# Moving eight pieces of one-time work within the first steps and the last steps of a cross-attention and quantised-FFN kernel

## The chip, the cores and the metric

The kernel runs on one core of one Trainium2 chip. The metric is the device time of one execution in microseconds (us), and the times below are medians over several executions. The engines are named as the profile names them: PE is TensorE, DVE is VectorE, ACT is ScalarE, POOL is GpSimd, and SP is SyncE, which here only starts DMAs. Each engine runs its own list of instructions in order; engines meet only at semaphores.

## The reference

Sixteen batches of 128 tokens with 512 features go through one layer. Each batch has a context of 128 rows with 256 features, of which the first 112 are the main context and the last 16 a second segment (DCA) with weights and a softmax of its own.

```python
x = x + xattn(layernorm(x), ctx)
x = x + ffn(layernorm(x), kernel, bias)

def xattn(x, y):                      # 16 heads of 32
    y_main, y_dca = y[:, :-16], y[:, -16:]
    kv_dca = y_dca @ Wkv_dca + bkv_dca
    k_dca, v_dca = ln(kv_dca[k half] per head), kv_dca[v half]
    q = ln((x @ Wq + bq) per head)
    k, v = ln((y_main @ Wk + bk) per head), y_main @ Wv + bv
    ctx = softmax(q k^T * SCALE) v + softmax(q k_dca^T * SCALE) v_dca
    return ctx @ Wo + bo

def ffn(x, kernel, bias):             # fake_quant: scale by max |.| / 127, round, scale back
    y = fake_quant(x, -1) @ fake_quant(kernel, 0) + fake_quant(bias, -1)
    return fake_quant(relu(y), -1)
```

## The kernel before, in words

**Steps.** Every engine's list is written by hand as a function `step` that is called for t = -3 to 17. In step t six batches are in work at once, each in another stage: L = t+3 (statistics of the first layernorm), A = t+2 (transposes and the products for k, q and v), N = t+1 (norm of the heads, the stacks of q and k for the scores), Bt = t (scores, maxima, exponentials, product with v), C = t-1 (output projection, second layernorm, FFN product) and D = t-2 (end of the FFN and the store). The names in the code are these letters; `A.first()` is true in step -2 alone, `N.first()` in step -1, `Bt.first()` in step 0, `C.first()` in step 1, and `final(Bt)` in step 15. From step 2 on every step is alike.

**One-time work.** Functions named `setup_...` prepare weights and constants and are called from the first steps, between the work of the batches. The change touches these:

- `setup_selectors` (ACT) copies `sel_rows` into `sel`, 128 rows of ones and zeros for each head, by which PE adds the right row of the negated maxima to the scores. PE waits for `sel_made` as the first thing of step 0.
- squares of q: ACT squares `q_raw` of batch A into `q_sq` (L843), DVE sums them by head (L1094, `qss_ready`) and turns the sums into means (L1129); ACT then takes -1/2 powers by a logarithm and an exponential (`heads`, L705 and L707), and DVE refines them (L1038 to L1041) and scales k and q (L1142 and L1146).
- `setup_columns` (ACT, L658) takes the magnitudes of two quarters of the FFN kernel; `setup_heads` (ACT, L679 and L681) is the -1/2 power for the DCA keys, `setup_scales` and `setup_dca` on DVE (L989) go on with it.
- `setup_ffn_bias` (DVE, L1015 to L1019) quantises the FFN bias in `fb_row`. It is first needed at L1238 in step 2.
- `setup_ffn(half)` (DVE, L1026 and L1027) makes one half of the FFN kernel into integers; `low_output` (DVE, L923) makes the low part of Wo, and `low_query` (L1121) the low part of q.
- `biased_keys` (DVE, L1103) adds the bias to the product for k and writes `k_raw`, for which ACT's `squared_keys` (L734) waits. In step 0, ACT's `expo(2)` (L750) stands behind that.
- `transposed_maxima` and `first_shifted` (PE, L1519, and L1433 with L1434) turn the maxima of batch Bt over and make its shifted scores for two groups of heads; ACT copies the turned maxima into `maxT` in between.
- `turn_over(into, n)` (PE, L1341) multiplies an identity n times into a bank that nobody reads.

**Products.** An FP32 product is three products of high and low parts (`split_product`, L1330): for q over four chunks, which is twelve matmuls of 512 columns, in two halves of six; for k and v over two chunks, six matmuls.

**Order within a step, PE.** Scores of groups 2 and 3 of Bt, output projection of C (L1330, `wo_hi` and `cT_hi`), transposes of k and q of N (L1507, L1512), product for k of A, maxima, first half of the product for q, shifted scores, second half, then `weigh` (L1453) and the rest of the shifted scores by turns, the FFN's transposes and product of C (L1587, L1617), scores of groups 0 and 1 of N (L1422), the transposes of the context (L1627), and the product for v of A.

## Time and profile before

| | |
|---|---|
| median of 3 runs | 357.25 us (355.57 to 361.37) |
| profiled execution | 358.21 us, of which the span of the trace is 356.4 us |
| PE busy | 326.6 us (92% of the span) |
| DVE busy | 314.6 us (88%) |
| ACT busy | 222.0 us (62%) |
| POOL busy | 173.9 us (49%) |
| mean granted TensorE clock | 0.971 |

The span runs from the first to the last instruction in the trace. A busy share is a mean over stages that have different limits, so it doesn't say which engine sets the time in a given step. The granted clock is that of TensorE, 1.0 for 2.4 GHz and 0.5 for 1.2 GHz.

### The profile page before, as it was taken

How to read it: one execution, taken by the hardware profiler on the slowest of the kernel's cores; microseconds unless marked ns; L12 is line 12 of the kernel's file. 1: busy time of each engine (PE TensorE's matmuls, PEld its weight loads, DVE VectorE, ACT ScalarE, POOL GpSimd, SP SyncE). 2: the span in 40 equal slices, each digit the busy share in tenths (PEclk: the TensorE clock that was granted, in tenths of full speed). 3: DMA queues.
4: the chain of work that ended last, by engine and by line, in shares of the span. 5: the costliest groups of instructions: out<-in, count | busy, mean ns of one | idle time of the engine just before them, and what ended most of it. 6: DMA issues, size and time to landing. Idle time of an engine off the chain costs nothing.

```text
span 356.4 us, 7623 instructions
## 1 busy us (share of the span) xinstructions
PE 326.6 (92%) x2372; PEld 257.8 (72%) x2372; DVE 314.6 (88%) x804; ACT 222.0 (62%) x444; POOL 173.9 (49%) x261
## 2 busy tenths in 40 slices
PE   6697879899999999999999999999999999987871
PEld 2354657778888878787878787878787878775640
DVE  2997998889989999999999999999999999986665
ACT  3357986356585858585858585858585856472401
POOL 6211613317282828282828383837373747372720
PEclk9999998699999999999999999999999999999895
DMA  7970334304241514242424242333333323230002
GB/s 259 272 286 3 103 111 151 115 14 136 49 148 48 175 50 149 76 159 67 151 76 147 77 137 90 125 103 118 109 120 106 121 63 120 63 125 25 30 1 88
DMA packets 36451, 38.88 MB, mean 109 GB/s; under 512 B 8760, under 2 KB 27452, under 8 KB 36412
## 3 DMA queue, kind: packets, MB, share of 16 engines
q1 hardware_dynamic: 36044, 38.14, 33.0%
q8 instruction: 19, 0.31, 0.4%
q10 hardware_dynamic: 368, 0.27, 0.3%
q14 instruction: 20, 0.16, 0.2%
HBM read 16.89 MB, written 4.72 MB: 61 GB/s over the span
## 4 chain that ended last, share of the span: by engine, by line
PE 60%; POOL 8%; DVE 5%; issue 4%; ACT 2%; DMA 1%; POOLq 0%; ACTq 0%; DVEq 0%
PE bank L1330 33%; PE bank L1453 9%; POOL finals L536 5%; PE bank L1433 3%; PE bank L1627 3%; PE bank L1434 3%; PE bank L1422 2%; PE bank L1617 2%; PE bank L1474 2%; PE bank L1507 2%; PE bank L1512 1%; POOL x_small L593 1%; DVE seg_out L1075 1%; ACT prob_store L750 1%; DVE rden L1069 1%
## 5 line engine op out<-in xcount | busy, mean ns | idle before, releaser
L517 POOL TENSOR_TENSOR k_lo<-wkv_raw,k_hi 128x448 f16<-128x448 f32 x16 | 16.8, 1047 | 110.5 <-issue 92.9
L1453 PE MATMUL bank<-v_aug,prob_store 128*128 128x66 f32 x512 | 67.9, 276 | 2.7 <-ACT prob_store L750 2.7
L1453 PEld LDWEIGHTS bank<-v_aug,prob_store 128*128 128x128 f32 x512 | 63.7, 193 | 5.2 <-ACT prob_store L750 4.0
L761 ACT ACTIVATE wkv_raw<-bank,affine 128x448 f32<-128x448 f32 (+1 forms) x32 | 22.6, 749 | 40.6 <-PE bank L1507 40.2
L1062 DVE TENSOR_REDUCE neg_max<-bank 128x4 f32<-128x448 f32 (+1 forms) x128 | 44.9, 412 | 0.3 <-PE bank L1422 0.3
L750 ACT ACTIVATE prob_store<-bank,exp_scale 128x512 f32<-128x512 f32 x64 | 41.6, 678 | 4.9 <-PE bank L1434 4.8
L536 POOL TENSOR_TENSOR finals<-seg_out 128x128 f32<-128x128 f32 x64 | 34.5, 547 | 12.5 <-DVE seg_out L1075 11.9
L1433 PE MATMUL bank<-q_stack,k_stack 128*128 128x128 f16 x256 | 33.9, 220 | 0.6 <-ACT maxT L612 0.6
L1434 PE MATMUL bank<-maxT,sel 128*128 128x128 bf16 x256 | 33.7, 219 | 0.0
L1075 DVE TENSOR_TENSOR seg_out<-bank,rden 128x256 f32<-128x256 f32 x64 | 27.2, 424 | 4.0 <-POOL finals L536 1.7
L1433 PEld LDWEIGHTS bank<-q_stack,k_stack 128*128 128x128 f16 x256 | 26.4, 104 | 5.2 <-issue 3.9
L1330 PE MATMUL bank<-wo_hi,cT_hi 128*128 128x512 f32 x64 | 26.7, 416 | 1.8 <-DVE cT_lo L1086 1.2
L1330 PE MATMUL bank<-wq_hi,xT_hi 128*128 128x512 f32 x64 | 27.7, 432 | 0.0
L1330 PE MATMUL bank<-wq_lo,xT_hi 128*128 128x512 f32 x64 | 25.3, 396 | 0.0
L1330 PE MATMUL bank<-wo_lo,cT_hi 128*128 128x512 f32 x64 | 25.3, 395 | 0.0
L1330 PE MATMUL bank<-wo_hi,cT_lo 128*128 128x512 f32 x64 | 25.3, 395 | 0.0
L1330 PE MATMUL bank<-wq_hi,xT_lo 128*128 128x512 f32 x64 | 25.2, 394 | 0.0
L1434 PEld LDWEIGHTS bank<-maxT,sel 128*128 128x128 bf16 x256 | 25.1, 98 | 0.0
L1094 DVE TENSOR_REDUCE qk_ss<-wkv_raw 112x16 f32<-112x512 f32 (+1 forms) x32 | 21.6, 677 | 2.2 <-ACT wkv_raw L843 1.9
L546 POOL TENSOR_TENSOR wq_raw<-wq_raw,fk_scale 128x512 f32<-128x512 f32 x15 | 19.3, 1286 | 6.4 <-ACT wq_raw L866 6.4
L734 ACT ACTIVATE wkv_raw<-k_raw 112x512 f32<-112x512 f32 x16 | 10.1, 631 | 19.3 <-DVE k_raw L1103 19.3
L1422 PE MATMUL bank<-k_stack,q_stack 128*128 128x128 f16 x256 | 20.3, 224 | 0.6 <-issue 0.6
(213 smaller groups left out, 893.7 us busy)
## 6 DMA issues: line engine op xcount, KB each, us to landing
x_in<-in_x SPq DMA_DIRECT2D x16, 256.0 KB, 3.2
q_stack<-q_hi SPq DMA_DIRECT2D x32, 128.0 KB, 2.1
q_stack<-q_lo SPq DMA_DIRECT2D x32, 128.0 KB, 2.1
k_stack<-k_hi SPq DMA_DIRECT2D x32, 128.0 KB, 2.1
k_stack<-k_lo SPq DMA_DIRECT2D x32, 128.0 KB, 2.1
out<-finals SPq DMA_DIRECT2D x16, 256.0 KB, 2.0
y_dcaT<-in_x SPq DMA_DIRECT2D x8, 256.0 KB, 2.9
x_res<-in_x SPq DMA_DIRECT2D x8, 256.0 KB, 2.8
```

The costliest lines, as they stand in the source:

```text
L536: g.tensor_tensor(ctx_out[:, HG * gr:HG * (gr + 1)], seg_out[:, gr % 2, :, 0], seg_out[:, gr % 2, :, 1], ALU.add).then_inc(ctx_ready.sem, 1)
L546: g.tensor_tensor(f_z, f_z, fk_scale[:], ALU.mult).then_inc(zs_ready.sem, 1)
L750: s.activation(flat(probs[:, gr % 2]), bank[4 + gr % 2][:, :], ACT.Exp, scale=exp_scale[:, 0:1]).then_inc(probs_ready.sem, 1)
L761: s.activation(n.rearrange("p (c n) -> p c n", n=P)[:, :, 0:keys], src, ACT.Identity, bias=shift, scale=gain).then_inc(n_ready.sem, 1)
L1062: v.tensor_reduce(neg_max[:, HG * gr:HG * (gr + 1), seg], s4[:, :, lo:hi], AX.X, ALU.max, negate=True).then_inc(max_ready.sem, 1)
L1075: v.tensor_tensor(seg_out[:, gr % 2], pv[:, :, 0:2 * HD].rearrange("p h (s d) -> p h s d", d=HD), rden[:, gr % 2].unsqueeze(3).to_broadcas ...
L1094: v.tensor_reduce(qk_ss[0:rows, n], grouped(sq[0:rows]), AX.X, ALU.add).then_inc(done.sem, 1)
L1330: last = mm(dst, a[:, c, 0:m], w[:, c, :], start=first, stop=c == end and a is xT_l)
L1422: last = mm(bank[4 + gr % 2][:, P * h:P * (h + 1)], q_stack[:, b.parity, h, gr], k_stack[:, b.parity, h, gr], start=True, stop=True)
L1433: mm(at, k_stack[:, Bt.parity, h, gr], q_stack[:, Bt.parity, h, gr], start=True, stop=False)
L1434: last = mm(at, sel[:, hh], maxT[:], start=False, stop=True)
L1453: last = mm(bank[6 + gr % 2][:, VW * h:VW * (h + 1)], probs[:, gr % 2, h], v_aug[:, Bt.parity, HG * gr + h], start=True, stop=True)
```

## The change

Nothing is computed in another way, and no instruction is added but three matmuls of an identity. Moved are:

1. ACT: the selectors, from the end of step -1 to step -2, between the copy of `y_dcaT` and the copies of `wq_hi`.
2. ACT, step -2: the squares of q and `setup_heads` go ahead of the magnitudes of the FFN kernel.
3. DVE, step -2: `biased_keys` goes ahead of `setup_norms` and `setup_affine`.
4. DVE: the FFN bias, from step 0 (ahead of `yT_lo`) to the end of step 1, ahead of the maxima of groups 0 and 1.
5. DVE, step 0: `setup_ffn(0)` goes ahead of `low_query` and `low_output`.
6. PE, step 0: `transposed_maxima` goes ahead of the first half of the product for q, and `first_shifted` ahead of the second half, as in the later steps.
7. PE, step 15: `turn_over(bank[3], 3)` behind `weigh(2)`.

```diff
             def setup_weights():
                 ...
                 setup_transposed()
+                setup_selectors()
                 for half in range(2):
                     act.wait_ge(wq_centred.sem, half + 1)
...
+                def squared_queries():
+                    act.wait_ge(*qraw_ready.of(A))
+                    if A.has(1):
+                        act.wait_ge(*qss_ready.of(A.back(1)))
+                    s.activation(q_sq, q_raw[:, A.parity], ACT.Square).then_inc(qsq_ready.sem, 1)
...
                         setup_squares()
                         squared_keys()
                         token_statistics()
+                        squared_queries()
+                        setup_heads()
                         setup_columns()
-                        setup_heads()
...
-                if A is not None:
-                    act.wait_ge(*qraw_ready.of(A))
-                    if A.has(1):
-                        act.wait_ge(*qss_ready.of(A.back(1)))
-                    s.activation(q_sq, q_raw[:, A.parity], ACT.Square).then_inc(qsq_ready.sem, 1)
+                if A is not None and not A.first():
+                    squared_queries()
                 if N is not None and N.first():
                     heads(A)
                     setup_wo()
                     setup_values()
                     setup_ffn()
-                    setup_selectors()
...
-                if Bt is not None and Bt.first():
-                    setup_ffn_bias()
...
                     if A.first():
                         low_queries()
+                        biased_keys()
                         setup_norms()
                         setup_affine()
-                        biased_keys()
                         setup_squares()
                 if Bt is not None and Bt.first():
+                    setup_ffn(0)
                     low_query()
                     low_output()
-                    setup_ffn(0)
...
                         head_products(A)
+                    if C is not None and C.first():
+                        setup_ffn_bias()
                     maxima(0)
                     maxima(1)
...
-                if Bt is not None and not Bt.first():
+                if Bt is not None:
                     transposed_maxima()
...
-                if Bt is not None and Bt.first():
-                    transposed_maxima()
-                if Bt is not None and not Bt.first():
+                if Bt is not None:
                     first_shifted()
...
-                if Bt is not None and Bt.first():
-                    first_shifted()
...
                     weigh(2)
+                    if final(Bt):
+                        turn_over(bank[3], 3)
```

ACT at the end of step -2 and the start of step -1, before the change. `x_norm,x_small` is the first of the three instructions of the token statistics; a line number of the changed kernel is up to seven higher for the same statement.

```order
L718 ACTIVATE x_norm,x_small<-x_in 128x512
L721 ACTIVATE x_norm,x_square<-x_in,x_small 128x512
L724 ACTIVATE x_small<-x_square,epsilon 128x1
L658 ACTIVATE prob_store<-fk_raw 128x512 x2
L679 ACTIVATE dca_small<-dca_small 128x32
L681 ACTIVATE dca_small<-dca_small 128x32
L843 ACTIVATE wkv_raw<-q_raw 128x512
L705 ACTIVATE qk_small<-qk_small 128x32
L707 ACTIVATE qk_small<-qk_small 128x32
```

The same place after the change.

```order
L719 ACTIVATE x_norm,x_small<-x_in 128x512
L722 ACTIVATE x_norm,x_square<-x_in,x_small 128x512
L725 ACTIVATE x_small<-x_square,epsilon 128x1
L741 ACTIVATE wkv_raw<-q_raw 128x512
L680 ACTIVATE dca_small<-dca_small 128x32
L682 ACTIVATE dca_small<-dca_small 128x32
L659 ACTIVATE prob_store<-fk_raw 128x512 x2
L706 ACTIVATE qk_small<-qk_small 128x32
L708 ACTIVATE qk_small<-qk_small 128x32
```

The square of q (`wkv_raw<-q_raw`) and the two instructions on `dca_small` now stand ahead of the magnitudes of `fk_raw`, and all of them stay ahead of the two of `heads` on `qk_small`.

DVE in step 0 before the change, from the last two instructions on the FFN bias on.

```order
L1018 TENSOR_SCALAR fb_row<-fb_row,fb_stat 128x512
L1019 TENSOR_SCALAR fb_row<-fb_row,fb_stat 128x512
L1086 TENSOR_TENSOR yT_lo<-y_in,yT_hi 128x224
L1086 TENSOR_TENSOR xT_lo<-bank0,xT_hi 128x512
L1062 TENSOR_REDUCE neg_max<-bank4 128x4 x2
L1062 TENSOR_REDUCE neg_max<-bank5 128x4 x2
L1186 CAST max_parts<-neg_max 128x32
L1188 TENSOR_TENSOR max_parts<-neg_max,max_parts 128x32
L1121 TENSOR_TENSOR q_lo<-wkv_raw,q_hi 128x512
L923 TENSOR_TENSOR wo_lo<-wo_raw,wo_hi 128x2048
L1026 TENSOR_TENSOR fk_raw<-fk_raw,fk_inv 128x1024
L1027 TENSOR_SCALAR fk_int<-fk_raw 128x1024
```

The same place after the change, behind the maxima of groups 0 and 1 of step -1, up to the sum for `k_raw`.

```order
L1090 TENSOR_TENSOR yT_lo<-y_in,yT_hi 128x224
L1090 TENSOR_TENSOR xT_lo<-bank0,xT_hi 128x512
L1066 TENSOR_REDUCE neg_max<-bank4 128x4 x2
L1066 TENSOR_REDUCE neg_max<-bank5 128x4 x2
L1188 CAST max_parts<-neg_max 128x32
L1190 TENSOR_TENSOR max_parts<-neg_max,max_parts 128x32
L1030 TENSOR_TENSOR fk_raw<-fk_raw,fk_inv 128x1024
L1031 TENSOR_SCALAR fk_int<-fk_raw 128x1024
L1125 TENSOR_TENSOR q_lo<-wkv_raw,q_hi 128x512
L927 TENSOR_TENSOR wo_lo<-wo_raw,wo_hi 128x2048
L1107 TENSOR_TENSOR k_raw<-bank3,bias_full 112x512
```

The FFN bias is gone from the front, and the half of the FFN kernel stands directly behind the maxima.

DVE at the change from step 1 to step 2 before, from the sum of the squares of q to the low part of the context.

```order
L1094 TENSOR_REDUCE qk_ss<-wkv_raw 128x16
L1062 TENSOR_REDUCE neg_max<-bank4 128x4 x2
L1062 TENSOR_REDUCE neg_max<-bank5 128x4 x2
L1129 TENSOR_SCALAR qk_small<-qk_ss 128x32
L1086 TENSOR_TENSOR cT_lo<-bank6,cT_hi 128x512
```

The same place after the change.

```order
L1098 TENSOR_REDUCE qk_ss<-wkv_raw 128x16
L1019 TENSOR_REDUCE fb_stat<-fb_row 128x1
L1020 TENSOR_SCALAR fb_stat<-fb_stat 128x1
L1021 RECIPROCAL fb_stat<-fb_stat 128x1
L1022 TENSOR_SCALAR fb_row<-fb_row,fb_stat 128x512
L1023 TENSOR_SCALAR fb_row<-fb_row,fb_stat 128x512
L1066 TENSOR_REDUCE neg_max<-bank4 128x4 x2
L1066 TENSOR_REDUCE neg_max<-bank5 128x4 x2
L1133 TENSOR_SCALAR qk_small<-qk_ss 128x32
L1090 TENSOR_TENSOR cT_lo<-bank6,cT_hi 128x512
```

The five instructions on the FFN bias stand between the sum of the squares and the maxima.

## Rows read from the trace of the kernel before

**Rows 1.** The chain of waits, by engine, from the page.

```profile
PE 60%; POOL 8%; DVE 5%; issue 4%; ACT 2%; DMA 1%; POOLq 0%; ACTq 0%; DVEq 0%
```

**Rows 2.** One steady step: start:end, length, busy PE, PEld, DVE, ACT, POOL, clock, DMA.

```profile
127.84:145.90 18.06, 17.81 (x143) 14.97 (x142) 17.17 (x47) 12.73 (x28) 10.42 (x15) 1.00 0.35 111
```

**Rows 3.** Timeline, ACT, steps -2 and -1: start, us, instruction, idle before it.

```profile
20.00 2.19 ACT L612 ACTIVATE wq_hi<-wq_raw 128x1024 fp32r<-128x1024 f32 x2 [4.91 <-DVE wq_raw L905]
...
29.11 1.13 ACT L658 ACTIVATE prob_store<-fk_raw 128x512 f32<-128x512 f32 x2
...
30.53 0.61 ACT L843 ACTIVATE wkv_raw<-q_raw 128x512 f32<-128x512 f32 x1
...
49.46 2.02 ACT L612 ACTIVATE sel<-sel_rows 128x1792 bf16<-128x1792 bf16 x2
```

**Rows 4.** Timeline, DVE, steps -2 and -1.

```profile
31.17 0.69 DVE L1094 TENSOR_REDUCE qk_ss<-wkv_raw 128x16 f32<-128x512 f32 x1 [1.89 <-ACT wkv_raw L843]
...
33.70 0.19 DVE L1038 SCALAR_TENSOR_TENSOR qk_small<-qk_small 128x32 f32<-128x32 f32 x1
```

**Rows 5.** Timeline, PE: steps -2, 0, 0, 2, 15 and 16.

```profile
28.85 3.60 PE L1409 MATMUL bank<-wo_raw,bv_sum 128*128 128x512 f32 x8
...
51.53 0.66 PE L1474 MATMUL bank<-ident,x_norm 128*128 128x128 f32 x4 [1.94 <-ACT sel L612]
...
64.64 2.66 PE L1453 MATMUL bank<-v_aug,prob_store 128*128 128x66 f32 x16 [1.05 <-ACT prob_store L750]
...
91.76 0.48 PE L1330 MATMUL bank<-wo_hi,cT_hi 128*128 128x512 f32 x1
...
333.95 0.40 PE L1587 MATMUL bank<-identb,f_int 128*128 128x128 bf16 x4 [0.69 <-ACT f_int L831]
...
341.68 2.41 PE L1341 MATMUL bank<-identb 128*128 128x512 bf16 x9
```

**Rows 6.** Timeline, DVE, step 0.

```profile
50.21 0.68 DVE L1015 TENSOR_REDUCE fb_stat<-fb_row 128x1 f32<-128x512 f32 x1
...
51.84 0.49 DVE L1019 TENSOR_SCALAR fb_row<-fb_row,fb_stat 128x512 f32<-128x512 f32 x1
...
56.47 1.12 DVE L1121 TENSOR_TENSOR q_lo<-wkv_raw,q_hi 128x512 f16<-128x512 f32 x1 [1.16 <-ACT q_hi L612]
57.52 3.38 DVE L923 TENSOR_TENSOR wo_lo<-wo_raw,wo_hi 128x2048 fp32r<-128x2048 f32 x1
...
62.06 0.69 DVE L1027 TENSOR_SCALAR fk_int<-fk_raw 128x1024 bf16<-128x1024 f32 x1
62.67 0.68 DVE L1103 TENSOR_TENSOR k_raw<-bank,bias_full 112x512 f32<-112x512 f32 x1
```

**Rows 7.** Timeline, DVE, step 1 and the start of step 2.

```profile
81.42 1.07 DVE L1027 TENSOR_SCALAR fk_int<-fk_raw 128x1024 bf16<-128x1024 f32 x1
...
88.93 1.41 DVE L1062 TENSOR_REDUCE neg_max<-bank 128x4 f32<-128x448 f32 x4
...
90.75 0.69 DVE L1086 TENSOR_TENSOR cT_lo<-bank,cT_hi 128x512 fp32r<-128x512 f32 x1
```

**Rows 8.** Timeline, POOL: step 1, step 2, and the last context part in step 15.

```profile
80.65 1.30 POOL L508 TENSOR_SCALAR wo_raw<-fk_raw,f_small 128x512 f32<-128x512 f32 x1
...
89.38 1.30 POOL L546 TENSOR_TENSOR wq_raw<-wq_raw,fk_scale 128x512 f32<-128x512 f32 x1 [0.43 <-ACT wq_raw L866]
...
336.46 0.89 POOL L536 TENSOR_TENSOR finals<-seg_out 128x128 f32<-128x128 f32 x1 [0.62 <-DVE seg_out L1075]
```

**Rows 9.** Busy time of stretches in steps 0 and 1, columns as in rows 2.

```profile
52.00:54.00 2.00, 2.00 (x17) 1.99 (x16) 1.86 (x5) 1.06 (x3) 0.00 (x0) 0.53 0.42 83
...
66.00:68.00 2.00, 2.00 (x15) 1.90 (x14) 1.04 (x4) 0.00 (x0) 1.33 (x3) 0.50 0.00 0
...
72.00:74.00 2.00, 2.00 (x17) 1.78 (x16) 2.00 (x4) 1.36 (x3) 0.00 (x0) 0.85 0.00 0
```

**Rows 10.** The same view near the end, steps 15 and 16.

```profile
336.00:338.00 2.00, 2.00 (x7) 0.76 (x5) 1.04 (x2) 0.87 (x2) 0.89 (x1) 0.50 0.03 12
```

More of the change, by code:

```diff
@@ L637, in setup_transposed, with setup_selectors @@
                 copy(y_dcaT[:].rearrange("p j c n -> p (j c n)"), bank[7][:, :]).then_inc(ydcaT_copied.sem, 1)
+            def setup_selectors():
+                act.wait_ge(rows_selected.sem, 1)
+                for seg, lo, hi in ((0, 0, MAIN), (1, MAIN, P)):
+                    copy(sel[:, :, lo:hi], sel_rows[:].rearrange("p (h s) -> p h s", s=2)[:, :, seg:seg + 1]
+                         .to_broadcast([P, H, hi - lo])).then_inc(sel_made.sem, 1)
             def setup_weights():
```

5 lines of the change are left out of this document (removed).

## The prediction

> **What bounds the kernel now.** I read three views. The chain of waits puts 60% of the span on PE [rows 1], so what delays PE anywhere is mostly kept to the end. The busy times of one steady step show the same more sharply: PE is busy 17.81 of 18.06 us [rows 2], and a stall that PE takes in one step is not won back in a later one, nor is a gain lost there. The change touches no steady step but the passage from step 1 to step 2, so the whole question is by how much PE enters the steady steps earlier, and what the last steps do. For that I read the timelines of ACT, DVE and PE up to 92 us side by side, asking at each idle of PE who came last, and who at each idle of that one. Three places come out. In step -2 the sum over q on DVE waits 1.89 us for ACT's squares [rows 4]. At the start of step 0 PE stands 1.94 us until ACT has written the selectors [rows 5]. Later in step 0 PE waits 1.05 us for an exponential [rows 5], which on ACT stands behind the squares of k, and those wait for `k_raw` from DVE at 62.67 [rows 6]: DVE bounds step 0, at its end at least.
>
> **Squares of q first (step -2), -1.7 us.** ACT now does the two magnitudes of the FFN kernel, 1.13 us from 29.11 on, and `setup_heads` before the squares at 30.53 [rows 3]. With the squares first they start 1.4 us earlier, and up to 1.9 us of DVE's wait [rows 4] can go, as DVE is busy until 29.3. Behind it DVE runs without a stop from the means to the scaled k, so the refinement at 33.70 [rows 4] moves with it. Next late would be ACT's powers for q and k (L705): they come behind the magnitudes now, at about 29.3 + 0.6 + 0.4 + 1.1 = 31.4, ready near 31.9, when DVE, which has the DCA scaling ahead of them, comes to need them. Next late after that is PE, whose product for the output bias ends at 32.45 [rows 5]; the first transposes it then owes are ready by 32, so PE holds back some tenths. I take 1.7 between 1.4 and 1.9. `biased_keys` ahead of the norms makes `k_raw` 1.9 us earlier and the affine columns 0.6 us later; PE needs these only in the output bias product at 28.85 [rows 5], which has 2 us to spare. That edit is zero in itself; it only lets ACT have the squares of k done in time. If the cover went, it would cost its 0.6.
>
> **Selectors and FFN bias out of step 0, -1.9 us together.** The selectors take ACT 2.02 us at 49.46 [rows 3]. In the new place ACT is idle for 4.91 us ahead of `wq_hi` [rows 3], so they cost nothing there; if that idle time were gone, `wq_hi` and with it the product for q would be late by 2 us. PE's wait of 1.94 us [rows 5] goes entirely, since the copy of `fk_inv` it needs as well ends just as the selectors begin. DVE has to follow, or nothing is won. It spends 50.21 to 52.33 on the FFN bias [rows 6], 2.12 us, just the time in which ACT is at the selectors. Without either, DVE gets the high part of y 3.6 us earlier (1.7 and 1.9). The two edits are one gain: each alone would leave the other as the bound.
>
> **Half of the FFN kernel ahead of `q_lo` (step 0), -1.1 us.** DVE waits 1.16 us for `q_hi` ahead of `q_lo` at 56.47 [rows 6], while the 1.85 us of `setup_ffn(0)` stand behind it. Put first, they fill this wait, and `k_raw` comes another 1.1 us earlier, at 58.0 in place of 62.67: -4.7 us in all. `q_lo` itself comes 0.7 us later against its neighbours; SP still has it stacked some 3 us before PE wants the scores of batch 1. POOL's work moves beside other instructions of DVE, which may shift some tenths either way. PE's order in step 0 (maxima before the first half of the product for q) gives ACT the turned maxima and so the first two exponentials sooner. I cost it at zero: PE then only waits longer for the third exponential, as `k_raw` is later than all of that. If DVE were not the bound, it would give up to 1.4 us, the six matmuls it steps ahead of.
>
> **FFN bias at the end of step 1, +2.0 us.** There it stands ahead of the maxima at 88.93 and so of the low part of the context at 90.75 [rows 7], without which PE's output projection, which started at 91.76 [rows 5], can't. The low part ended at 91.4, so 0.3 of the 2.12 us is slack: +1.8. In step 0 POOL was idle beside it. Here POOL has its product with `fk_scale` from 89.38 to 90.68 [rows 8], just where the two 512-wide instructions fall. A row on such company: `fk_int` took 0.69 us alone [rows 6] and 1.07 us beside POOL's L508 [rows 7, 8], 0.4 more. That is +2.2 as the upper value; a gap of 0.3 between the means and the low part of the context may close, which is +1.5. I take 2.0. Behind PE at that point are the transposes of k and q and all of step 2, which is why it is kept.
>
> The Trainium skill, "SBUF — State Buffer", on the shared port pair, says that a DVE instruction in a two-port mode or with two SBUF inputs and a GpSimd one exclude each other, and whichever comes second is blocked for the whole of the other. By that rule the fourth instruction on the bias would wait for POOL's product to end, about 0.65 us, and this term would be 2.4 and the sum -2.4. The longer row of `fk_int` agrees in sign; it shows 0.4, not a block for the whole 1.30 us.
>
> **Identity products in step 15, -0.1 us.** Nine of them took 2.41 us [rows 5], so three take 0.8 us with their end, in an idle time of 0.69 us [rows 5], the last 0.1 of it being overlap: no delay. What they could give is the clock: it was 0.50 at 336 to 338 us [rows 10]. But the projection of the last batch waits there for the last part of the context, which POOL finishes at 337.35 [rows 8], whatever PE's clock. At most 0.6 us, at least -0.1 (a late transpose); I take 0.1.
>
> **Sum.** -1.7 - 1.9 - 1.1 + 2.0 - 0.1 = -2.8 us. On the profiled execution's own 358.2 us that is 355.4. That execution lies 1.0 us above the median of 357.25, so I forecast 354.5. With every term at its ends it is -4.0 to -1.7. A measurement of this kernel can tell a difference of about 2% (7 us) from none, so this is "same".
>
> **Rivals.**
>
> *The clock falls in step 2 (0.20).* PE idles about 2 us there in three pieces. After the 1.94 us at the start of step 0 the granted clock was at the lower level of 1.2 GHz (0.53 over 52 to 54 [rows 9]), at which each microsecond of work costs half a microsecond more than it should. Such a stretch costs 0.9 us at least, and the long one after the wait at 64.64, more than 6 us of which 66 to 68 and 72 to 74 are shown [rows 9], 3.3. I take 1.7: sum -1.1, 356.2. Against it: between the pieces PE has dense products. The Trainium skill, "TensorE: Matmul & The Clock Gate", says in its part on the clock gate that a recently idle array gets half its pulses; by that the fall is possible in each such place, and it names none.
>
> *The clock stays up after step 0 (0.15).* The long stretch of 66 to 73 us [rows 9] follows the wait at 64.64 [rows 5]. With the selectors' stall gone, PE is busier before it. Then step 1 gains; PE alone would gain 3.3, but DVE, hardly idle there, lets 2.1 through: sum -4.9, 352.3. Against it: the wait at 64.64 grows, since PE arrives earlier than DVE.
>
> *The first term does not arrive (0.10).* The change then doesn't do what it says for step -2: PE's output bias product until 32.45 [rows 5] and ACT's list behind it take the place of the squares as the last to come, and 0.3 of 1.7 is left: sum -1.4, 355.9.
>
> *Slower (0.05).* The stall in step 2 brings the lower clock for as long as the one at 64.64 did: +3.3 on the sum, +0.5 against before, 357.7. It decides from a low stretch of over 5.6 us on, all of it PE's.
>
> **Chances and range.** The forecast has 0.50. The range reaches from the case with the clock up and the terms near their good ends (351.5) almost to the slower case (357.5). More than 2% faster would need over 7 us, which no case gives but in chance with the spread of the runs (355.57 to 361.37): 0.04. More than 2% slower has no mechanism: 0.02. The rest is 0.94.
>
> **What would show it.** In the profile after: the second sum of squares on DVE at 29.3 to 29.8 with hardly an idle; PE into step 0 at about 48 with no wait for `sel`; `k_raw` of step 0 at about 58; PE's third `weigh` at about 60 with an idle time of over 1 us ahead of it; in step 2 PE's first `wo_hi` product at 89.1, waiting for `cT_lo`, and the bias's 512-wide instructions longer than 0.49 us. The steady step stays at 18.06. It is wrong if `k_raw` is waited for by nobody in step 0, if the clock in step 2 is below 1, or if step 2's stall is under 1 us.

## The result, and the profile after

The changed kernel takes 354.8 us in the median of 11 runs (353.72 to 357.25), the kernel before 358.02 in 11 runs beside them; the ratio is 0.9925 [0.9896, 0.9953]. A second set of 12 runs gave 355.01 against 358.53, ratio 0.9947 [0.9909, 0.9984]; two of the 29 runs of the kernel before in that set were slow ones (360.25 and 361.54), which the ratio and the comparison of single runs below leave out. That is 0.5 to 0.8% faster by the ratios (0.9 to 1.0% by the medians), "same" by the 2% bound, and the forecast of 354.5 is met. The profiled span went from 356.4 to 353.0 us. The number came out right with two of its terms wrong and with TensorE's clock as a third cause, to which the forecast gave nothing; the rest of this text is about that.

The chain of waits by engine, kernel after (answers to [rows 1]):

```profile
PE 59%; POOL 8%; DVE 7%; issue 5%; ACT 2%; DMA 1%; POOLq 0%; DVEq 0%; ACTq 0%
```

PE still carries it, so the starts of PE's landmarks tell where time was won. The timeline of PE, kernel after (start, us, instruction, idle time before it and who ended it; answers to [rows 5]):

```profile
48.07 0.63 PE L1478 MATMUL bank<-ident,x_norm 128*128 128x128 f32 x4 [0.26 <-ACT fk_inv L612]
...
52.80 0.22 PE L1523 MATMUL bank<-identb,max_parts 128*128 128x128 bf16 x1 [1.45 <-DVE max_parts L1190]
...
60.36 2.00 PE L1457 MATMUL bank<-v_aug,prob_store 128*128 128x66 f32 x16 [0.83 <-ACT prob_store L757]
...
85.43 0.40 PE L1426 MATMUL bank<-k_stack,q_stack 128*128 128x128 f16 x4 [0.74 <-DVE neg_max L1066]
86.09 0.40 PE L1426 MATMUL bank<-k_stack,q_stack 128*128 128x128 f16 x4 [0.27 <-DVE neg_max L1066]
86.99 0.64 PE L1334 MATMUL bank<-wo_hi,cT_hi 128*128 128x512 f32 x1 [0.50 <-DVE cT_lo L1090]
...
335.60 0.47 PE L1334 MATMUL bank<-wo_hi,cT_hi 128*128 128x512 f32 x1 [0.88 <-DVE cT_lo L1162]
```

The reader sees the selectors' wait of 1.94 gone (0.26 is left), PE in step 0 at 48.07 in place of 51.53, the third `weigh` at 60.36 in place of 64.64, and three new idle times in step 2, 1.51 us together. DVE in steps -2 and 0, kernel after (answers to [rows 4, 6]):

```profile
28.42 1.47 DVE L1098 TENSOR_REDUCE qk_ss<-wkv_raw 112x16 f32<-112x512 f32 x2
...
31.74 0.19 DVE L1042 SCALAR_TENSOR_TENSOR qk_small<-qk_small 128x32 f32<-128x32 f32 x1
...
51.63 1.02 DVE L1190 TENSOR_TENSOR max_parts<-neg_max,max_parts 128x32 bf16<-128x32 f32 x1
52.57 2.36 DVE L1030 TENSOR_TENSOR fk_raw<-fk_raw,fk_inv 128x1024 f32<-128x1024 f32 x1
...
58.38 0.68 DVE L1107 TENSOR_TENSOR k_raw<-bank,bias_full 112x512 f32<-112x512 f32 x1
```

Both sums of squares of step -2 run without idle and the refinement comes 1.96 us earlier. `k_raw` of step 0 comes 4.29 us earlier. Two instructions there are long (`max_parts` 1.02, `fk_raw` 2.36), and POOL was busy beside them. POOL in steps 0 and 2, kernel after; the second row is its sum of x and the output bias, which stands in the buffer named `y_dca`:

```profile
51.57 1.03 POOL L517 TENSOR_TENSOR k_lo<-wkv_raw,k_hi 128x448 f16<-128x448 f32 x1 [7.29 <-issue]
52.56 1.29 POOL L583 TENSOR_TENSOR y_dca<-y_dcaT,out_bias 128x512 f32<-128x512 f32 x1
...
82.59 1.29 POOL L546 TENSOR_TENSOR wq_raw<-wq_raw,fk_scale 128x512 f32<-128x512 f32 x1 [0.42 <-ACT wq_raw L870]
```

DVE ahead of PE's idle times in step 2, kernel after (answers to [rows 7]):

```profile
82.14 0.68 DVE L1019 TENSOR_REDUCE fb_stat<-fb_row 128x1 f32<-128x512 f32 x1
...
83.24 0.92 DVE L1022 TENSOR_SCALAR fb_row<-fb_row,fb_stat 128x512 f32<-128x512 f32 x1
84.20 0.51 DVE L1023 TENSOR_SCALAR fb_row<-fb_row,fb_stat 128x512 f32<-128x512 f32 x1
84.63 1.40 DVE L1066 TENSOR_REDUCE neg_max<-bank 128x4 f32<-128x448 f32 x4
```

Last the clock. PE's busy time in stretches, kernel after (start:end, length, busy PE, granted clock, DMA share, GB/s; answers to [rows 9, 10]):

```profile
65.00:67.00 2.00, 2.00 (x19) 1.00 0.32 116
...
86.00:88.00 2.00, 1.40 (x7) 0.78 0.00 0
88.00:90.00 2.00, 2.00 (x7) 0.50 0.00 0
...
336.00:338.00 2.00, 2.00 (x10) 1.00 0.00 0
```

The lower level (1.2 GHz) after the third `weigh` of step 0 is gone; it appears in step 2, behind the new idle times, and not at 336.

**The ledger.** The starts on PE of five landmarks cut the way into stages: k product of step -1 (B), transposes of x in step 0 (C), third `weigh` of step 0 (D), first output projection product of step 1 (E), of step 2 (F), of step 16 (G). "Wait" is the idle time ahead of D. All from PE's timeline of each profiled execution, us, with the kernels of the experiments below in the same table:

| kernel | B | B to C | C to D | wait | D to E | E to F | F to G |
|---|---|---|---|---|---|---|---|
| before | 38.22 | 13.31 | 13.11 | 1.05 | 8.55 | 18.57 | 246.97 |
| after | 36.30 | 11.77 | 12.29 | 0.83 | 6.05 | 20.58 | 248.61 |
| changed_again | 38.37 | 11.86 | 12.11 | 0.65 | 6.07 | 20.59 | 247.01 |
| squares_alone | 37.03 | 13.55 | 12.39 | 0.37 | 6.06 | 18.55 | 247.30 |
| selectors_alone | 38.21 | 12.56 | 12.62 | 0.56 | 6.06 | 18.54 | 247.55 |
| bias_alone | 38.32 | 14.27 | 12.30 | 1.67 | 8.57 | 20.61 | 247.32 |
| all_but_bias | 36.56 | 11.67 | 12.75 | 0 | 6.07 | 18.56 | 247.27 |
| fk_behind | 37.10 | 11.88 | 12.24 | 0.77 | 6.05 | 20.59 | 247.07 |
| clock_held | 36.27 | 11.65 | 12.28 | 0.81 | 6.06 | 20.58 | 246.72 |
| sum_later | 36.77 | 11.85 | 11.31 | 0 | 6.08 | 20.59 | 247.14 |
| bias_back_sum_later | 37.33 | 11.83 | 11.92 | 0 | 6.06 | 18.54 | 247.06 |
| pe_order_back | 36.69 | 11.87 | 12.13 | 1.52 | 8.55 | 20.59 | 247.14 |
| no_identities | 36.28 | 11.63 | 12.11 | 0.65 | 6.07 | 20.59 | 247.11 |
| bias_on_gpsimd | 36.59 | 11.67 | 11.67 | 0.60 | 6.07 | 18.55 | 247.11 |

From before to after: -1.92 (B), -1.54 and -0.82 (step 0), -2.50 (D to E), +2.01 (E to F), +1.64 (F to G, of which 1.52 lies between F and the next k product), and -0.27 behind G, together -3.40, the difference of the spans. Two of these are clock: D to E holds the same work in 6.05 us at 1.00 and in 8.55 with the clock mostly at 0.50, and 1.52 of the +1.64 is the fall in step 2. Most of the -0.82 is clock too, as squares_alone will show.

### The profile page after: what moved, and what is told of

It is laid out like the page before. It is cut to its first block, busy times and chain, and to the rows that moved or that the text cites. A ratio compares the mean times of both kernels' runs of the same rounds, so it can differ in the third digit from the quotient of the medians.

```text
span 353.0 us, 7629 instructions
## 1 busy us (share of the span) xinstructions
PE 321.9 (91%) x2375; PEld 254.4 (72%) x2375; DVE 315.7 (89%) x804; ACT 221.9 (63%) x444; POOL 173.8 (49%) x261
## 4 chain that ended last, share of the span: by engine, by line
PE 59%; POOL 8%; DVE 7%; issue 5%; ACT 2%; DMA 1%; POOLq 0%; DVEq 0%; ACTq 0%
PE bank L1334 33%; PE bank L1457 9%; POOL finals L536 5%; PE bank L1437 3%; PE bank L1438 3%; PE bank L1629 2%; PE bank L1426 2%; PE bank L1511 2%; PE bank L1516 1%; PE bank L1478 1%; POOL x_small L593 1%; DVE seg_out L1079 1%; PE bank L1619 1%; DVE rden L1073 1%; ACT prob_store L757 1%
## 5 line engine op out<-in xcount | busy, mean ns | idle before, releaser
L1457 PE MATMUL bank<-v_aug,prob_store 128*128 128x66 f32 x512 | 67.1, 274 | 2.1 <-ACT prob_store L757 2.1
```

The source lines that it names most:

```text
L1457: last = mm(bank[6 + gr % 2][:, VW * h:VW * (h + 1)], probs[:, gr % 2, h], v_aug[:, Bt.parity, HG * gr + h], start=True, stop=True)
```

## The experiments

The first four were timed against 29 runs of the kernel before (357.5 us), the next four against 23 (356.16), the last four against 29 (358.53). Where I compare medians they are of kernels timed together, or I give both ratios.

**squares_alone**: the kernel before with the squares of q first in step -2 and the keys ahead of the norms.

```diff
                         token_statistics()
+                        squared_queries()
+                        setup_heads()
                         setup_columns()
-                        setup_heads()
```

> The kernel before with two edits alone: ACT squares q of step -2 ahead of the magnitudes of the FFN kernel, and DVE adds the bias to k ahead of the norms. Theory (the wait for the squares set step -1): the sum over q on DVE has hardly an idle, PE's product for k of step -1 starts 1.9 us earlier (36.3 in place of 38.2), PE still stands some 1.9 us at the start of step 0 for the selectors, and the whole is 1.7 to 1.9 us faster. Rival (something else comes last in step -1, PE's output bias product or ACT's list behind it): under 0.5 us.

355.27 us, ratio 0.9932 [0.9893, 0.9971]. PE's timeline in step 0:

```profile
50.58 0.66 PE L1478 MATMUL bank<-ident,x_norm 128*128 128x128 f32 x4 [1.93 <-ACT sel L612]
...
62.97 2.00 PE L1457 MATMUL bank<-v_aug,prob_store 128*128 128x66 f32 x16 [0.37 <-ACT prob_store L756]
```

B is at 37.03 and the selectors' wait stands unchanged at 1.93: the term is independent of the others. The median is 2.2 us below that of before, where 1.7 to 1.9 was expected, but D to E is 6.06 in this execution, so some of that may be clock.

This run also shows what made step 0 of the kernel before longer in its profiled execution. Step 0 holds the same lists and the same selectors' wait in both, and yet DVE's wait for `q_hi` is 0.45 here and was 1.16 there. PE and then ACT, kernel before:

```profile
52.77 0.95 PE L1507 MATMUL bank<-ident,wq_raw 112*128 112x112 f32 x4
```

```profile
53.76 1.63 ACT L761 ACTIVATE wkv_raw<-bank,affine 128x448 f32<-128x448 f32 x2 [0.94 <-PE bank L1507]
```

The same for squares_alone, and its DVE:

```profile
51.52 0.56 PE L1511 MATMUL bank<-ident,wq_raw 112*128 112x112 f32 x4
```

```profile
52.11 1.62 ACT L767 ACTIVATE wkv_raw<-bank,affine 128x448 f32<-128x448 f32 x2 [0.24 <-PE bank L1511]
```

```profile
54.80 1.12 DVE L1125 TENSOR_TENSOR q_lo<-wkv_raw,q_hi 128x512 f16<-128x512 f32 x1 [0.45 <-ACT q_hi L612]
```

In the kernel before the clock had fallen (0.53 over 52 to 54 us) by the time of the transposes of k. They took 0.95 us in place of 0.56, ACT waited 0.94 in place of 0.24, and `q_hi`, `q_lo`, `k_raw` and the third `weigh` each came 0.7 us later behind the start of step 0 (C to D 13.11 against 12.39). In squares_alone the clock fell as well (0.50 over 52 to 54 us), but behind those transposes. So 0.7 of the 1.16 us, and 0.7 of the 1.05 us ahead of D, were the clock. Over all kernels with this edit B lies at 36.27 to 38.37, the middle one at 36.69, and at 38.21 to 38.32 in the three without.

**selectors_alone**: the kernel before with `setup_selectors()` behind `setup_transposed()` alone.

```diff
                 setup_transposed()
+                setup_selectors()
...
                     setup_ffn()
-                    setup_selectors()
```

> The kernel before with one edit alone: the selectors are written in step -2. Theory (DVE is the bound of step 0 once PE's wait is gone, since the FFN bias still keeps it until 52.3): PE starts step 0 about 1.6 to 1.9 us earlier, but the k_raw of step 0 on DVE stays within 0.5 us of 62.7, and the time within 0.5 us of before as long as the granted clock does the same; PE just waits longer for the third exponential. Rival (PE's wait was the bound): k_raw at about 60.8 and the whole 1.9 us faster. If the clock does not fall at the start of step 1 any more, up to 2.5 us come off in either case, and then only the place of k_raw decides between the two.

354.45 us, ratio 0.9915 [0.9883, 0.9948]: 3.0 us below the median of before, of which D to E (6.06) is 2.5 in the profiled executions. DVE has no wait for `q_hi`, and `k_raw` is at 61.41 in place of 62.67, beyond the 0.5 us that were expected. B to D is 25.18 against 26.42, and against 25.94 in squares_alone, where the clock did not make the transposes late: 0.8 us less with the FFN bias still in step 0, and that with a mean clock of 0.91 over 30 to 48 us. So this edit alone earns something, and the forecast's "each alone would leave the other as the bound" falls.

**bias_alone**: the kernel before with only the FFN bias moved to the end of step 1.

```diff
-                if Bt is not None and Bt.first():
-                    setup_ffn_bias()
...
+                    if C is not None and C.first():
+                        setup_ffn_bias()
                     maxima(0)
```

> The kernel before with one edit alone: the FFN bias goes from step 0 to the end of step 1. Theory (in step 0 DVE then waits for ACT, which is at the selectors, so nothing is won there; at the end of step 1 it delays the low part of the context): k_raw of step 0 stays within 0.5 us of 62.7, PE's output projection of step 2 waits about 2 us, and the whole is 2.0 us slower, up to 3.6 if the clock falls in that wait. Rival (each edit earns its own time): k_raw 2 us earlier, and the whole within 0.5 us of before.

359.68 us, ratio 1.0049 [1.0007, 1.009]: slower beyond the interval, "same" by the 2% bound. B to D is 26.57, with a clock of 0.50 to 0.94 over 36 to 42 us in it, and E to F is 20.61 in place of 18.57. DVE ahead of the low part of y, and PE at the third `weigh`:

```profile
53.40 0.39 DVE L1086 TENSOR_TENSOR yT_lo<-y_in,yT_hi 128x224 fp32r<-128x224 f32 x1 [1.98 <-issue]
```

```profile
64.89 3.53 PE L1453 MATMUL bank<-v_aug,prob_store 128*128 128x66 f32 x16 [1.67 <-ACT prob_store L750]
```

With the selectors still there, the 2.12 us that DVE saves come back as 1.98 of waiting. This half of the forecast's sentence is true: the bias alone earns nothing in step 0 and costs 2.0 in step 2.

**all_but_bias**: the changed kernel with the bias back in step 0.

```diff
+                if Bt is not None and Bt.first():
+                    setup_ffn_bias()
...
-                    if C is not None and C.first():
-                        setup_ffn_bias()
                     maxima(0)
```

> The changed kernel with the FFN bias back in step 0. Theory: the k_raw of step 0 comes 1.9 to 2.1 us later than in the changed kernel (60.4 in place of 58.4), and in return PE's output projection of step 2 has no wait and no low clock behind it; the time is that of the changed kernel, within 0.7 us, if the clock does not fall in step 2 there, and up to 1.6 us faster than it where it does. Rival (moving the bias is what made the change faster): 1.5 us or more slower than the changed kernel.

352.46 us in 6 runs, ratio 0.9857 [0.9808, 0.9907]: 2.3 us below the changed kernel's first median (ratio 0.9925 [0.9896, 0.9953]), where at most 1.6 was expected. DVE in step 0:

```profile
48.62 0.65 DVE L1019 TENSOR_REDUCE fb_stat<-fb_row 128x1 f32<-128x512 f32 x1
...
52.95 1.08 DVE L1190 CAST max_parts<-neg_max 128x32 bf16<-128x32 f32 x1
54.07 0.19 DVE L1192 TENSOR_TENSOR max_parts<-neg_max,max_parts 128x32 bf16<-128x32 f32 x1
54.18 1.22 DVE L1030 TENSOR_TENSOR fk_raw<-fk_raw,fk_inv 128x1024 f32<-128x1024 f32 x1
...
58.84 0.68 DVE L1107 TENSOR_TENSOR k_raw<-bank,bias_full 112x512 f32<-112x512 f32 x1
```

`k_raw` is only 0.46 later than in the changed kernel, with 2 us more work ahead of it, where 1.9 to 2.1 later was expected. The difference is in the rows: DVE is free of its waits ahead of the low parts of y and x (0.23 and 0.17 in the changed kernel), and POOL costs it less. POOL's `k_lo` falls beside the maxima, which read a bank and take 1.41 us with it or without; its sum falls beside the cast (1.08), and `setup_ffn`'s first instruction comes after it and takes 1.22. That is 0.90 us of company, against 1.98 in the changed kernel (`max_parts` 1.02 and `fk_raw` 2.36). B to D is 24.42, so of the 2.4 us between the profiles of before and after the bias's move gives 0.4 and selectors, order and clock 2.0; measured from squares_alone (25.94), where the clock had not made step 0 late, it is 0.4 of 1.9. In step 2 E to F is 18.56.

**fk_behind**: the changed kernel with `setup_ffn(0)` behind `low_output()` again.

```diff
-                    setup_ffn(0)
                     low_query()
                     low_output()
+                    setup_ffn(0)
```

> The changed kernel with the first half of the FFN kernel back behind the low parts of q and wo (edit 5 undone). Theory (the wait for q_hi is filled by it): DVE waits about 1 us for q_hi again, the raw keys of step 0 come 0.9 to 1.1 us later than 58.4, and since PE waits for the third exponential behind them (0.83 us idle ahead of its third weigh in the changed kernel), PE leaves step 0 0.9 to 1.1 us later: about +1.0 us. Rival (the wait for q_hi had already been closed by the selectors' move, as it had in the run with the selectors alone, where the stretch from the bias to the raw keys was 10.24 us against 12.46): the raw keys move by under 0.4 us and the time by 0 to 0.4.

354.84 us, ratio 0.9942 [0.9908, 0.9975], the same as the changed kernel's two. The rival holds. DVE, then POOL, in step 0:

```profile
53.48 0.68 DVE L1125 TENSOR_TENSOR q_lo<-wkv_raw,q_hi 128x512 f16<-128x512 f32 x1
54.09 3.38 DVE L927 TENSOR_TENSOR wo_lo<-wo_raw,wo_hi 128x2048 fp32r<-128x2048 f32 x1
57.39 1.21 DVE L1030 TENSOR_TENSOR fk_raw<-fk_raw,fk_inv 128x1024 f32<-128x1024 f32 x1
```

```profile
53.47 1.85 POOL L583 TENSOR_TENSOR y_dca<-y_dcaT,out_bias 128x512 f32<-128x512 f32 x1
```

There is no wait for `q_hi` to fill. From the low part of y to `k_raw` it takes 9.54 us here (49.71 to 59.25) and 9.57 in the changed kernel (48.81 to 58.38). Which instruction stands beside POOL's sum changes, `wo_lo` 3.38 or `fk_raw` 2.36 (2.28 and 1.21 without it), and not what it costs.

**clock_held**: the changed kernel with six identity matmuls in step 2's idle times.

```diff
+                    if D is not None and D.first():
+                        pe.wait_ge(*qraw_ready.of(N))
+                        turn_over(bank[2], 3)
...
+                    if D is not None and D.first():
+                        turn_over(bank[2], 3)
```

> The changed kernel with six extra identity matmuls on PE in step 2, three ahead of the scores and three behind the last of them, so that PE does something in the 1.5 us in which it otherwise waits for the maxima and the low part of the context. They cost no time if they end before what PE waits for comes. Theory (the stall has two prices, its own 2.0 us and the low clock behind it): the granted clock stays at 1.00 from 86 to 91 us, the first output projection product still starts at about 87, and PE leaves step 2 some 1.6 us earlier than in a run in which the clock fell; in the medians -0.5 to -1.6, since the clock does not fall there in every execution. Rival (the clock falls all the same, or does not depend on these idle stretches): no difference, or up to 0.5 us slower by the extra matmuls.

353.35 us, ratio 0.9882 [0.9833, 0.9931]. The timeline of PE in step 2:

```profile
84.40 0.81 PE L1345 MATMUL bank<-identb 128*128 128x512 bf16 x3
...
86.17 0.81 PE L1345 MATMUL bank<-identb 128*128 128x512 bf16 x3
86.84 0.47 PE L1334 MATMUL bank<-wo_hi,cT_hi 128*128 128x512 f32 x1
```

They cost nothing and the clock was 1.00 from 84 to 91 us. But it was so too, without them, in the profiled executions of changed_again, fk_behind, sum_later, pe_order_back and no_identities, which have the same idle times: of six without the matmuls one lost the clock, the first. Its median is 1.5 us below that of fk_behind, with overlapping intervals and 6 runs. That is in the direction of the theory and doesn't show it; this stays open.

**sum_later**: the changed kernel with POOL's sum of x and the output bias for the first batch behind its last product of step 0.

```diff
-                if Bt is not None:
-                    if Bt.first():
-                        pool.wait_ge(out_bias_ready.sem, 1)
+                if Bt is not None and not Bt.first():
...
                     combine(3)
+                if Bt is not None and Bt.first():
+                    pool.wait_ge(out_bias_ready.sem, 1)
+                    pool.wait_ge(*xres_loaded.of(Bt))
+                    g.tensor_tensor(x_plus, x_res[Bt.parity], out_bias[:], ALU.add).then_inc(xplus_ready.sem, 1)
```

> The changed kernel with the sum of x and the output bias of the first batch, which GpSimd does for 1.3 us from 52.56 in step 0, moved behind its last product of the step. Theory (DVE lost 1.15 us in step 0 because its 512-wide cast L1190 took 1.02 instead of 0.19 and its instruction L1030 took 2.36 instead of 1.21 beside GpSimd): L1030 is back at about 1.2, the raw keys come 0.9 to 1.2 us earlier than 58.4, and the third weigh starts earlier by what was its wait (up to 0.8 us): -0.5 to -0.8 us in the whole. The cast stays long, as what stands beside it is another GpSimd instruction. Rival (the length of L1030 is not GpSimd's doing): L1030 stays at 2.3 and nothing moves.

354.34 us, ratio 0.9925 [0.9893, 0.9958]. DVE in step 0 (the line was L1030):

```profile
53.13 1.21 DVE L1032 TENSOR_TENSOR fk_raw<-fk_raw,fk_inv 128x1024 f32<-128x1024 f32 x1
...
57.78 0.69 DVE L1109 TENSOR_TENSOR k_raw<-bank,bias_full 112x512 f32<-112x512 f32 x1
```

1.21 again, 8.39 us from the low part of y (49.39) to `k_raw` in place of 9.57, no wait at D, and C to D 11.31 in place of 12.29 and 12.11. The 32-wide instruction that stays long at 1.02 (`max_parts`, which the expectation calls a 512-wide cast) stands beside `k_lo`, as expected. The profile shows the 0.8 to 1.0 us; the medians, 0.5 below that of fk_behind, can't confirm it.

**bias_back_sum_later**: both, bias in step 0 and POOL's sum later.

> The changed kernel with the FFN bias back in step 0 (352.46 us median before in another call, 2.3 us faster than the changed kernel) and GpSimd's sum of x and the output bias moved behind its last product of step 0. Theory (with the bias in step 0 DVE comes last there, and each instruction that GpSimd lengthens is on the path): the raw keys come up to 0.9 us earlier than 58.84, PE's waits ahead of the product for k and the third weigh shrink, 0.4 to 0.9 us faster than 352.46: about 351.8, no stall in step 2. Rival (PE is the bound of step 0 there, as it did not idle ahead of the third weigh in that run): no difference from 352.5.

351.59 us (351.31 to 352.8) in 6 runs, ratio 0.9838 [0.9789, 0.9887], the fastest here, and "unclear" by the 2% bound, since the interval crosses it. C to D is 11.92 against 12.75 in all_but_bias, and step 2 has no stall. Against sum_later the bias in step 0 costs 0.61 us (11.92 to 11.31) and saves 2.05 in step 2.

**changed_again**: the changed kernel unaltered.

> The changed kernel once more, unaltered, as the measure for the three beside it and to see whether the clock falls in step 2 again. Theory (the fall after the stall there comes in some executions only, since two kernels with the same stall kept the clock at 1.00 from 84 to 91 us and one lost it): 353.7 to 355 us in the median, with single times up to 357; if its profiled execution keeps the clock in step 2, that step's first output projection product comes at about 87 and the next product for k 1.6 us earlier against it than the 5.15 us of the first profile. Rival (it falls in this kernel always): 0.50 to 0.80 between 86 and 91 us again.

355.01 us. PE's busy time in stretches of step 2, columns as above:

```profile
88.00:90.00 2.00, 1.39 (x8) 1.00 0.00 0
90.00:92.00 2.00, 2.00 (x11) 1.00 0.00 0
```

The same stall, E to F 20.59, and the clock stayed up. This execution lost it elsewhere, 0.68 between 20 and 24 us, and its B is 2.1 us later than the first's.

**pe_order_back**: the changed kernel with PE's order of before in step 0.

```diff
-                if Bt is not None:
+                if Bt is not None and not Bt.first():
                     transposed_maxima()
...
+                if Bt is not None and Bt.first():
+                    transposed_maxima()
...
+                if Bt is not None and Bt.first():
+                    first_shifted()
```

> The changed kernel with PE's order in step 0 put back (edit 6 undone: the turned maxima and the first shifted scores behind the product for q, as before). Theory (cost zero, as PE waits for the third exponential anyway, which hangs on the raw keys): the first exponential comes 1.4 us later against the start of step 0, the wait of 0.83 us ahead of the third weigh shrinks or goes, PE's wait of 1.45 us ahead of the turned maxima goes, since the product for q stands there; the time changes by 0 to +0.6. Rival (the order is what lets PE follow DVE; without it PE's chain through the exponentials is the bound): the third weigh starts 0.8 to 1.4 us later and the kernel is that much slower.

356.10 us beside changed_again's 355.01, ratio 0.995 [0.9915, 0.9985]. C to D is the same (12.13 and 12.11), as the theory had it. But the time PE waits is not: the 1.45 us ahead of the turned maxima are gone and stand at D. The timeline of PE, pe_order_back:

```profile
60.69 3.06 PE L1457 MATMUL bank<-v_aug,prob_store 128*128 128x66 f32 x16 [1.52 <-ACT prob_store L757]
```

PE's busy time in the stretches behind it, columns as above:

```profile
60.00:62.00 2.00, 1.31 (x9) 0.85 0.79 210
62.00:64.00 2.00, 2.00 (x14) 0.50 0.15 58
```

D to E is 8.55 us, as in the kernel before. The wait was only moved on the line, yet the clock fell behind it. Neither theory had said that. It is one execution; the medians are 1.1 us apart in the same sense, but the ratios (0.995 and 0.9947) are not apart at all.

**no_identities**: the changed kernel without `turn_over(bank[3], 3)` in step 15.

```diff
                     weigh(2)
-                    if final(Bt):
-                        turn_over(bank[3], 3)
```

> The changed kernel without the three identity products in step 15 (edit 7 undone). Theory (they touch only the clock, and the last batch's projection waits for POOL, whatever the clock): the last output projection starts at the same place, 14.1 us behind that of step 15, and the clock falls to 0.5 somewhere between 332 and 338 us as in the kernel before, which makes the 12 products of the projection 1.3 us longer when it does; since what follows waits for them, +0.5 to +1.6 in such executions, 0 in the others. The prediction had put 0.1 on them. Rival (the clock there stays up without them): no difference.

354.37 us, ratio 0.9924 [0.989, 0.9957]. The last projection starts 14.08 us behind that of step 15 (319.71 to 333.79), as in the changed kernel (321.52 to 335.60), and the clock from 318 to 342 us was 1.00 without the identities. So the rival holds for this pair. Over all profiled executions it is less clear: of the five kernels without these identities, three (before, squares_alone, bias_alone) have a clock of 0.50 to 0.54 somewhere in the 5 us around the start of the last projection, and of the nine with them none. In squares_alone, where that lasted to 338 us, the way behind G is 19.1 us in place of 17.4. Whether the identities can save such a fall stays open.

**bias_on_gpsimd**: bias_back_sum_later with the bias's two 512-wide instructions on POOL.

```diff
-                link(v.tensor_scalar(fb_row[:], fb_row[:], fb_stat[:, 2:3], ROUND, ALU.mult, ALU.add))
+                g.tensor_scalar(fb_row[:], fb_row[:], fb_stat[:, 2:3], ROUND, ALU.mult, ALU.add
+                                ).then_inc(pool_steps.sem, 1)
```

> The fastest so far (FFN bias back in step 0, GpSimd's sum moved behind its last product; 351.59 us median in another call) with the two 512-wide instructions on the bias given to GpSimd, which is idle for 6.8 us ahead of its k_lo in step 0; VectorE keeps the maximum, the scale and its reciprocal. Theory (VectorE is what PE waits for, 1.02 us ahead of the product for k and 0.80 us ahead of the turned maxima): VectorE gets to the low part of y 0.9 us earlier, the raw keys come 0.6 to 0.9 us earlier against the start of step 0, and the third weigh 0.3 to 0.6: -0.3 to -0.6 us. Rival (what GpSimd does beside VectorE's two-input subtractions lengthens these by as much): the low part of y or of x takes over 1 us, and nothing is won.

352.34 us, ratio 0.9877 [0.9829, 0.9925], not faster than bias_back_sum_later (351.59, ratio 0.9838). C to D is 0.25 shorter (11.67). POOL's second instruction, and what then stood beside POOL's delayed `k_lo` on DVE:

```profile
50.73 2.01 POOL L493 TENSOR_SCALAR fb_row<-fb_row,fb_stat 128x512 f32<-128x512 f32 x1
```

```profile
54.31 1.52 DVE L1135 TENSOR_TENSOR q_lo<-wkv_raw,q_hi 128x512 f16<-128x512 f32 x1
```

Part of what DVE was spared it spent again beside POOL, 1.52 in place of 0.69 for `q_lo`.

## Why the forecast was right, and where it was not

**Squares of q first, -1.7.** Right: B moved by 1.92 in the profile, and by 1.5 from the three kernels without the edit to the middle of those with it. The sums of squares of step -2 run from 28.42 without idle, where 29.3 to 29.8 was named for the second.

**Selectors and FFN bias, -1.9 together; half of the FFN kernel, -1.1.** B to D won 2.36 (2.45 in changed_again) of these 3.0 us, 0.7 of it by the clock, and the working was wrong in both steps. The step that failed first is "DVE waits 1.16 us for `q_hi`", a wait that `setup_ffn(0)` was to fill for -1.1 us. That wait hung on the selectors' stall: 0.45 us of it stands behind the stall alone (squares_alone), and 0.7 is the low clock that followed the stall in that one execution. With the selectors moved it is gone before anything fills it (selectors_alone, fk_behind), so filling it earned 0; with only the bias moved DVE waits 1.98 us ahead of the low part of y instead (bias_alone). I counted one stall in two terms. The other failed step is "the two edits are one gain". The selectors earn nearly all of it without the bias (all_but_bias keeps all but 0.4). I had counted the bias's 2.12 us as a full gain for DVE; without the bias, DVE stood idle 0.40 us more and lost 1.1 us more beside POOL (1.98 against 0.90).

**FFN bias at the end of step 1, +2.0.** Right: E to F is 18.54 to 18.57 in the six kernels without it and 20.58 to 20.61 in the eight with it. The instructions took 2.49 us (82.14 to 84.63), 0.37 over 2.12, and 0.48 of slack was there, 0.28 ahead of the low part of the context (0.41 before, 0.13 after) and the rest ahead of PE. So this edit earns 0.4 and costs 2.0; it is the one to take back.

**PE's order, 0.** Wrong by the one profile that there is, though the reason given for it was right: PE does wait for the third exponential anyway. What it misses is that a wait has a second price. Split into 1.45 and 0.65 to 0.83 it left the clock at 1.00; in one piece of 1.52 behind one of 0.39 the clock fell to 0.50, which cost 2.5 us there. Whether that costs in most executions the times (1.1 us in the medians, nothing in the ratios) leave open.

**Identity products, -0.1.** 0 by no_identities, where the clock at 336 to 338 is up without them. That they never help isn't shown.

**The clock.** The forecast gave 0.15 to its staying up after step 0 and argued that the wait at the third `weigh` grows. Without the order edit it does grow, to 1.52, and the clock falls (pe_order_back). With it the wait is split, 0.83 and 0.65 are left at D, and D to E won 2.5 in both profiled executions of the changed kernel. The rival with a clock that falls in step 2 was given 0.20; it happened in one of the two, at 1.52 us where 1.7 was priced. Two of the prediction's own signs are therefore against it: the clock of 0.50 in step 2 in that execution, and the wait at the third `weigh`, which was to be over 1 us. In the execution that had both, the terms make -1.92 - 2.36 + 2.01 + 0.12 - 0.27 = -2.4, of which 0.7 is the late transposes; that leaves -1.7 for the moves, where -2.8 was forecast, and -1.7 for the clock (-0.7 - 2.50 + 1.52).

The single runs say how much of the medians is clock. Each comes with its mean granted clock, which follows how long the lower level lasted. Of the other 27 runs of the kernel before beside changed_again, 14 had 0.975 or less and took 356.3 to 360.0 us, and 4 had 0.990 or more; of the 12 of changed_again 9 had 0.990 or more and none was below 0.981. At equal clock the two are much closer: at 0.996 one run of 354.81 against two of 353.92 and 354.09, at 0.991 three of 355.53 to 355.58 against four of 354.55 to 355.24, with a median of 355.0. That is 0.5 to 0.8 us. Of the 3.2 to 3.5 us in the medians the greater part is therefore that the changed kernel holds the clock more often, not that its moves make the way shorter. The same view puts all_but_bias at 351.6 and 352.1 in its two runs at 0.995, some 2 us below the changed kernel at 0.996, as the 2.0 us that the bias's move costs would have it. And it names the edit that holds the clock: the median of the granted clock is 0.988 in selectors_alone, against 0.978 in squares_alone and in the kernel before beside both. So the median of 354.8 meets 354.5 by luck. The forecast took the clock as unchanged and all of the 2.8 us as moves; the moves gave less and the clock the rest. The mean clock doesn't say where a run lost it, and these are few runs, so the split is an estimate; why the clock falls in one execution and not in another stays open.

## What to carry to other kernels

When two engines wait in the same stretch, ask whether both waits come from one stall before adding up what filling each would give. Work moved to a new place costs its whole length if that engine is last there (2.0 us), and leaving the old place earns only what was not already idle or held up (0.4 of 2.1). Where a wait can't be removed, cutting it into two with work between may still pay, through the clock (2.5 us between two profiled executions). And before a difference of medians is put down to the moves, compare runs at equal granted clock: here 3.2 to 3.5 us became 0.5 to 0.8.

## What the runs showed that I had not expected

**POOL and DVE exclude each other, for some of DVE's instructions.** In pe_order_back the pair can be read off. POOL, then DVE:

```profile
53.07 2.36 POOL L583 TENSOR_TENSOR y_dca<-y_dcaT,out_bias 128x512 f32<-128x512 f32 x1
```

```profile
53.08 1.21 DVE L1030 TENSOR_TENSOR fk_raw<-fk_raw,fk_inv 128x1024 f32<-128x1024 f32 x1
54.33 1.66 DVE L1031 TENSOR_SCALAR fk_int<-fk_raw 128x1024 bf16<-128x1024 f32 x1
```

POOL's sum, 1.29 alone, starts beside DVE's 1.21 us instruction and is longer by 1.07; it then runs to 55.43, and DVE's next instruction, 0.69 alone, is longer by 0.97. A small one suffers as much: the 32-wide `max_parts` took 1.02 in place of 0.19 beside `k_lo`, and in all_but_bias the 32-wide cast 1.08 in place of 0.18 beside the sum. DVE's maxima, which read a bank, took 1.41 beside `k_lo` in all_but_bias and elsewhere without it. The Trainium skill, "SBUF — State Buffer", says in "SBUF: two separate sides" that of a DVE instruction in a two-port mode or with two SBUF inputs and a GpSimd one, whichever starts first has the shared pair for its whole instruction and the other fully blocks; these rows agree with the block. Which one is first, the rows can't foretell: POOL's sum and `fk_raw` start 0.01 us apart, POOL's ahead, in both profiled executions of the changed kernel, and in the first `fk_raw` was the one blocked (2.36), in changed_again the sum (2.37).

A blocked DVE instruction ends 0.13 to 0.15 us before the recorded end of POOL's plus its own time (`fk_raw` 2.36 where 1.28 and 1.21 make 2.49; `max_parts` 1.02 for 1.16; the cast 1.08 for 1.23). In step 2 `fb_row` at 83.24 began 0.64 us before the recorded end of POOL's product and took 0.92 where a whole block would make 1.13, so 0.21 less; `fk_int` in the kernel before, 1.07 where 0.53 were left of POOL's L508, would make 1.22 and is 0.15 less. The prediction read that row as "not a block for the whole 1.30 us"; with only 0.53 us left to block, it can't be told from one. By the page this term would have been 2.4, and it measured 2.0, for these tenths and for 0.48 of slack in place of 0.3.

**Where the clock fell.** Behind D it was at 0.50 in the three executions in which PE had waited 1.05, 1.52 and 1.67 us there, and at 1.00 in the eleven with 0.83 or less. In step 0 it fell behind the selectors' waits of 1.94 (before) and 1.93 (squares_alone) and not behind the 1.50 of bias_alone. In step 2 it fell in one execution of the changed kernel and not in the other, behind the same idle times; in the setup (0.68 from 20 to 24 us) it was the other one.
